# A layer norm, attention and int8 MLP block on one core: PV products of two key tiles at a time, two probability buffers, attended rows stored over the queries, and the output projection spread over the next batch's windows

## Chip, cores, metric

One NeuronCore of a Trainium2 chip runs one program. The metric is the device time of one execution in microseconds (us); three executions of the kernel before were timed, and one more was profiled. The engines are TensorE (PE in the rows; PEld is its weight loads), VectorE (DVE), ScalarE (ACT), GpSimd (POOL) and SyncE (SP), which issues the DMAs.

## What is computed

```python
x: (4, 512, 512) f32;  xn = layernorm(x)
# attention: 32 heads of 16, one key/value head shared by all
q = xn @ wq;  k = xn @ wk;  v = xn @ wv          # k, v: 16 wide
probs = softmax(causal(q @ k.T / 4))
s = (probs @ v) @ wo
# int8 MLP: columns of the input whose absolute maximum is over 3.0 stay out of the quantization;
# rows of the rest, and rows of W, are rounded to 127 steps of their own absmax
h = linear8bit(xn, W1, b1)                        # 512 -> 2048
g = silu(linear8bit(h, W2, b2))                   # 2048 -> 512
out = x + s * g
```

## The kernel before

All of it is one program with an instruction stream per engine, written out by hand; semaphores order them. An operand of a matmul that needs full precision is split into a high and a low half (fp32r), and a product is three matmuls: high by high, high by low, low by high. There are four stages.

1. Preparation (to about 92 us): layer norm, transposition of x, queries of all four batches into the tiles `big_h` and `big_l` (both halves, features by tokens, resident for the whole kernel), keys and values.
2. Attention (about 94 to 453 us), the stage of the change.
3. First MLP stage (L1046 on): W1 tiles are scaled, rounded and transposed; h = W1 by quantized x, in 16 feature tiles f of 4 chunks c of 512 tokens each. The quantized x overwrites `big_h` and `big_l`.
4. Second MLP stage and the output.

**Attention.** A unit u is one batch b and one strip f of 128 query features (8 heads of 16): U = 16 units, f = u mod 4. Time is counted in steps g (L747, L822, L961 loop over them on each engine), and CH = 24 steps make a window. Three things run staggered in it:
- Row maxima. `max_piece` (L878) computes the scores of unit u in 24 pieces, queries by keys, into three banks in turn; VectorE reduces each to its maxima (L838) and so frees the bank. After the 24th, `maxima` (L953) transposes the maxima into the miscellaneous bank MISCB (L957). ScalarE takes their high half (`mh`, L779), VectorE their low half (`ml`, L873), and SyncE puts both beneath the queries in `stack` (L660), so that the next score matmuls subtract the maxima.
- Scores and probabilities, one window later. `scores` (L901, L910) issues 22 matmuls per unit, keys by queries, 11 for each of two head parities p, with three banks; ScalarE takes the exponential into `probs` (L759), and GpSimd zeroes the masked corner after the last one of each key tile kt (L741). Key tile kt has 512 - 128 kt query columns.
- PV (L915, L922). Per parity and key tile, four matmuls with 32 weight columns each (values and ones) go side by side into the four column groups of the array and add into one bank, PVB, over the four key tiles. `PV_AT` says at which step of the unit each is issued. VectorE transposes the bank (L805, L811), takes reciprocals and transposes back (L819); GpSimd multiplies (L725). ScalarE and GpSimd store both halves of the attended rows (L767, L730) into `at_h`, `at_l`, which have five slots.

Since `probs` is one buffer, the exponentials of a parity wait for PV of the other parity before (L757).

**Output projection** (`project`, L938). For batch b, row tile j of 128 tokens is the sum over the four units k of the batch: three matmuls of 512 columns for each (j, k), a *projection step* below. Its bank is MISCB, the one that row maxima use; `misc_bank` (L927) has the first step of a row tile wait until the last user of the bank was taken: `maxima_low` (s_ml) after row maxima, `projected_evicted` (s_ob) after another row tile. `PROJECT_AT` (L556) lists the steps, counted from the batch's last unit; `PROJECT_LAST` that of the last batch, back to back after everything.

**The tail.** After the last piece (g = 384) tiles of the quantized x are loaded from DRAM (L680), transposed (L982) into the freed maxima banks, and their halves stored over the queries in `big_h`, `big_l` (L786, L852), every second step. EARLY = 15 of the 16 tiles are done so. The last one is done in the first MLP stage (`transpose_x` L1260, `high_x` L1117, `low_x` L1178) ahead of chunk 1 of f = 0.

In the first MLP stage the banks 4 to 7 serve all transposes in turn: `aux` (L1035) lists them, and the n-th waits until the one four before it was taken (`aux_bank`, L1252). In VectorE's order (L1213 on) come the low half of the first W1 tile, the scaling of the second, the scaling of W2's first 128 rows (`scale_w2`, L1186; a load of 1 MB), and then `low_x`. The code of the parts that the diff touches:

## Time and profile before

| | us |
|---|---|
| median of 3 executions | 870.93 (869.99 to 877.79) |
| profiled execution: time | 875.71 |
| profiled execution: span of its trace | 874.0 |
| TensorE busy (matmuls) | 799.8 (92%) |
| VectorE / ScalarE / GpSimd busy | 675.3 / 406.5 / 253.5 |
| mean granted TensorE clock | 0.966 of full speed |

Busy times are sums over the span; "idle before" in a row is the engine's idle time ahead of the instruction and what ended it. A matmul row's duration overlaps the next one's, so the cost of a matmul is read from its start to the next one's start. PEclk 1.00 is 2.4 GHz, 0.50 is 1.2 GHz.

### The profile page before, as it was taken

Reading aid. Unit: us, or ns where it says so; the run is one execution under the profiler, and the core shown is the slowest. Engines: PE = TensorE matmul, PEld = TensorE weight load, DVE = VectorE, ACT = ScalarE, POOL = GpSimd, SP = SyncE. Lnnn points to the kernel's source line nnn. Section 1 sums busy time; section 2 is a strip of 40 time slices with the busy share of each in tenths; the row PEclk is TensorE's granted clock in tenths of the full one; section 3 lists DMA queues with packets and bytes.
Section 4 is the critical chain, followed back from the end, with each engine's and each line's share of the span. In section 5 each row is a group of like instructions: output and inputs, shape, how many; then the busy total and the mean of one; then the engine's idle time right before and its main releaser. Section 6 shows DMA issues by size and latency. Waiting matters only on the chain. (4 is left out here: it accounts for less than half of the span.)

```text
span 874.0 us, 12108 instructions
## 1 busy us (share of the span) xinstructions
PE 799.8 (92%) x4253; PEld 579.6 (66%) x4253; DVE 675.3 (77%) x1116; ACT 406.5 (47%) x682; POOL 253.5 (29%) x331
## 2 busy tenths in 40 slices
PE   3899999999999999999889999999996999999983
PEld 2677655556655665566457878787875888887772
DVE  6898879897798789878535675765656998599967
ACT  2224056665666566666833455445444332143221
POOL 7101125454455445444441001010100000135306
PEclk9999679999999999999999999999997999999997
DMA  5721202322232222231534443412004234024852
GB/s 143 238 99 49 65 23 64 87 77 74 81 88 78 87 79 70 63 99 62 169 126 142 143 152 114 145 53 81 25 24 169 61 120 157 25 85 144 258 200 96
DMA packets 53884, 89.90 MB, mean 103 GB/s; under 512 B 10288, under 2 KB 18496, under 8 KB 52416
## 3 DMA queue, kind: packets, MB, share of 16 engines
q1 hardware_dynamic: 53824, 89.13, 32.6%
q8 instruction: 34, 0.56, 0.3%
q14 instruction: 26, 0.21, 0.1%
HBM read 47.69 MB, written 28.31 MB: 87 GB/s over the span
## 5 line engine op out<-in xcount | busy, mean ns | idle before, releaser
L838 DVE TENSOR_REDUCE rowmax<-ps 128x2 f32<-128x512 f32 (+3 forms) x384 | 215.5, 592 | 48.1 <-PE ps L897 46.4
L759 ACT ACTIVATE probs<-ps 128x512 f32<-128x512 f32 (+1 forms) x352 | 182.1, 559 | 115.2 <-PE ps L910 114.2
L897 PE MATMUL ps<-km,stack 128*128 128x256 f32 (+3 forms) x512 | 154.6, 357 | 2.4 <-PEq L171 1.9
L897 PEld LDWEIGHTS ps<-km,stack 128*128 128x128 f32 (+1 forms) x512 | 97.4, 200 | 71.0 <-DVE rowmax L838 44.4
L910 PE MATMUL ps<-stack,ks 128*128 128x512 f32 (+1 forms) x352 | 134.3, 389 | 9.6 <-DMA stack<-ml 9.6
L741 POOL TENSOR_SCALAR_AFFINE_SELECT probs<-probs 128x512 f32<-128x512 f32 x128 | 79.8, 635 | 115.5 <-ACT probs L759 115.5
L1631 PE MATMUL ps<-big_h 128*128 128x512 f32 x256 | 101.9, 398 | 9.1 <-DVE big_l L1556 9.1
L1303 PE MATMUL ps<-big_h,w1h 128*128 128x512 f32 x256 | 105.2, 411 | 1.4 <-DVE w1l L1174 1.4
L1305 PE MATMUL ps<-big_h,w1l 128*128 128x512 f32 x256 | 101.7, 397 | 0.0
L1304 PE MATMUL ps<-big_l,w1h 128*128 128x512 f32 x256 | 101.1, 395 | 0.0
L1633 PE MATMUL ps<-big_h,big_l 128*128 128x512 f32 x256 | 100.9, 394 | 0.0
L1632 PE MATMUL ps<-big_l,big_h 128*128 128x512 f32 x256 | 100.9, 394 | 0.0
L922 PE MATMUL ps<-probs,vones 128*32 128x512 f32 (+3 forms) x1024 | 95.5, 445 | 1.4 <-POOL probs L741 0.7
L910 PEld LDWEIGHTS ps<-stack,ks 128*128 128x128 f32 x352 | 66.9, 193 | 17.2 <-DMA stack<-ml 12.9
L1174 DVE TENSOR_TENSOR w1l<-ps,w1h 128x512 fp32r<-128x512 f32 x16 | 11.1, 692 | 71.2 <-ACT w1h L1114 71.2
L1631 PEld LDWEIGHTS ps<-big_h 128*128 128x128 f32 x256 | 48.8, 191 | 22.0 <-issue 11.9
L1491 ACT CAST big_h<-projected_rows 128x512 fp32r<-128x512 f32 x32 | 19.8, 618 | 88.1 <-DVE projected_rows L1529 65.2
L1305 PEld LDWEIGHTS ps<-big_h,w1l 128*128 128x128 f32 x256 | 48.4, 189 | 12.2
L1303 PEld LDWEIGHTS ps<-big_h,w1h 128*128 128x128 f32 x256 | 48.6, 190 | 11.7 <-DVE w1l L1174 1.6
L1633 PEld LDWEIGHTS ps<-big_h,big_l 128*128 128x128 f32 x256 | 48.8, 191 | 10.3
L1632 PEld LDWEIGHTS ps<-big_l,big_h 128*128 128x128 f32 x256 | 48.9, 191 | 10.0
L1304 PEld LDWEIGHTS ps<-big_l,w1h 128*128 128x128 f32 x256 | 48.6, 190 | 10.2
(193 smaller groups left out, 1286.1 us busy)
## 6 DMA issues: line engine op xcount, KB each, us to landing
stack<-big_h SPq DMA_DIRECT2D x128, 64.0 KB, 2.0
projected_rows<-w2t_scratch SPq DMA_DIRECT2D x32, 256.0 KB, 2.6
h_scratch<-hs SPq DMA_DIRECT2D x7, 1024.0 KB, 4.5
hload<-h_scratch SPq DMA_DIRECT2D x14, 512.0 KB, 5.0
xn_scratch<-xa SPq DMA_DIRECT2D x4, 1024.0 KB, 5.2
stack<-big_l SPq DMA_DIRECT2D x64, 64.0 KB, 2.0
xi<-xn_scratch SPq DMA_DIRECT2D x16, 256.0 KB, 2.7
xe_scratch<-xm SPq DMA_DIRECT2D x16, 256.0 KB, 2.3
```

The source lines that it names most:

```text
L741: nc.gpsimd.affine_select(out=d, in_=d, compare_op=ALU.is_ge, fill=0.0, base=0, pattern=[[0, NPAIR], [1, P]], channel_multiplier=-1).then_ ...
L759: nc.scalar.activation(probs[:, o:o + nh * w], ps[:, STB[n % NST], 0:nh * w], ACT.Exp).then_inc(s_exp, 1)
L838: nc.vector.tensor_reduce(dst, src, AX_X, ALU.max).then_inc(s_red, 1)
L897: last = nc.tensor.matmul(dst, stack[u % 3][rows, hp, P * qt:P * (qt + 1)], km[rows, u // KT, p0:p0 + npar, keys], start=True, stop=True)
L910: ins = nc.tensor.matmul(ps[:, STB[n % NST], 0:nh * w].rearrange("p (h q) -> p h q", h=nh), ks[:, u // KT, p, P * kt:P * (kt + 1)], stack[ ...
L922: ins = nc.tensor.matmul(ps[32 * j:32 * j + 32, PVB, P * kt:T], vones[:, u // KT, kt, :], probs[:, o:o + w], start=(kt == 0), stop=(kt == ...
L1303: nc.tensor.matmul(dst, w1h[f % 2][:, k, :], big_h[:, k, t], start=(k == 0), stop=False)
L1304: nc.tensor.matmul(dst, w1h[f % 2][:, k, :], big_l[:, k, t], start=False, stop=False)
L1305: last = nc.tensor.matmul(dst, w1l[f % 2][:, k, :], big_h[:, k, t], start=False, stop=(k == KT - 1))
L1631: nc.tensor.matmul(ps[:, i, :], hqh[m % RB][:, t], w2h[m % RB], start=(kk == 0), stop=False)
L1632: nc.tensor.matmul(ps[:, i, :], hqh[m % RB][:, t], w2l[m % RB], start=False, stop=False)
L1633: return nc.tensor.matmul(ps[:, i, :], hql[m % RB][:, t], w2h[m % RB], start=False, stop=(kk == FT - 1))
```

## The change

- PV takes two key tiles at a time: `GROUPS` = (0, 1), (2, 3). The eight issues of four matmuls per unit become four of eight, at steps 11, 16, 22, 27 of the unit where they were at 7, 11, 14, 16, 19, 21, 25, 27. The matmuls are the same.
- `probs` gets a second buffer, one for each parity; the exponentials wait for the PV of the same parity of the unit before.
- The attended rows are stored over the queries of their own unit in `big_h` and `big_l`; `at_h` and `at_l` go.
- The projection of batches 0 and 1 is spread over the four windows of the next batch, one row tile in each, at steps 3, 8, 13, 19 after T0. Batch 2 has its row tiles 0 and 1 in the last two windows with pieces, and its row tiles 2 and 3, every second step, in the tail.
- Because batch 3's attended rows stand where x tiles 12 to 15 would go, EARLY is 12: the tail does 12 tiles, and the first MLP stage four, two ahead of chunk 1 and two ahead of chunk 2. Their loads are issued two ahead of the weights' and two behind them.

The diff, cut to its core:

```diff
@@ tiles
-        probs = sa("probs", [P, NP_])
+        probs = [sa(f"probs{p}", [P, NP_]) for p in range(2)]
...
-        SLOTS = KT + 1
-        at_h = sa("at_h", [P, SLOTS, T], F32R)
-        at_l = sa("at_l", [P, SLOTS, T], F32R)
+        def attended(part, u):
+            b, f = divmod(u, KT)
+            return part[:, f, T * b:T * (b + 1)]
...
+        GROUPS = [(0, 1), (2, 3)]
+        NG = len(GROUPS)
@@ tables
-        PV_AT = {7: (0, 0), 11: (0, 1), 14: (0, 2), 16: (0, 3), 19: (1, 0), 21: (1, 1), 25: (1, 2), 27: (1, 3)}
+        PV_AT = {11: (0, 0), 16: (0, 1), 22: (1, 0), 27: (1, 1)}
...
-        T0 = CH + 11
-        PROJECT_AT = {t + T0: divmod(n, KT) for n, t in enumerate(
-            [-1, 1, 2, 3, 11, 12, 14, 15, 18, 20, 23, 24, 34, 35, 37, 39])}
+        T0 = 2 * CH + 2 - LAG
+        def spread_over(windows):
+            return {T0 + CH * w + at: (j, k) for j, (w, steps) in enumerate(windows) for k, at in enumerate(steps)}
+
+        EVENLY = (3, 8, 13, 19)
+        PROJECT_AT = spread_over([(j, EVENLY) for j in range(QT)])
+        PROJECT_NEXT_TO_LAST = spread_over([(0, EVENLY), (1, EVENLY), (2, (0, 2, 4, 6)), (2, (8, 10, 12, 14))])
...
-                table = PROJECT_AT if b + 1 < B else PROJECT_LAST
+                table = PROJECT_AT if b + 2 < B else PROJECT_NEXT_TO_LAST if b + 1 < B else PROJECT_LAST
...
-        EARLY = NT - 1
+        EARLY = NT - QT
@@ scalar, attention
-                        if 2 * u + p >= 1:
-                            act.wait_ge(s_pv, pv_count(u, p, kt) - 4)
+                        if u:
+                            act.wait_ge(s_pv, pv_count(u - 1, p, group_of(kt)))
...
-                        if u >= SLOTS:
-                            act.wait_ge(s_mf, misc_at[("o", (u - SLOTS) // KT, QT - 1)] + 1)
-                        nc.scalar.copy(at_h[:, u % SLOTS, :],
+                        nc.scalar.copy(attended(big_h, u),
@@ tensor, attention
-                def pv(u, p, kt):
-                    if kt == 0 and 2 * u + p:
+                def pv(u, p, group):
+                    if group == 0 and 2 * u + p:
                         pe.wait_ge(s_pvf, 2 * u + p)
-                    pe.wait_ge(s_msk, pv_count(u, p, kt))
-                    w = T - P * kt
-                    for j in range(NPAIR):
...
+                    for kt in GROUPS[group]:
+                        pe.wait_ge(s_msk, masked_count(u, p, kt))
+                        w = T - P * kt
+                        for j in range(NPAIR):
...
@@ first MLP stage
+        def late_x(f, c):
+            return range(EARLY + 2 * c - 2, EARLY + 2 * c) if f == 0 and c in (1, 2) else ()
...
-                if f == 0 and c == 1:
-                    aux += [("x", i) for i in range(EARLY, NT)]
+                aux += [("x", i) for i in late_x(f, c)]
...
-                for i in range(EARLY, NT):
-                    load_x(i)
+                load_x(EARLY)
+                load_x(EARLY + 1)
                 load_w1(1)
                 load_w1(2)
                 sp.dma_start(w2n[:, :], W2[0:P, :]).then_inc(s_w2n, 16)
+                for i in range(EARLY + 2, NT):
+                    load_x(i)
...
-                        if f == 0 and c == 1:
-                            for i in range(EARLY, NT):
-                                transpose_x(i)
+                        for i in late_x(f, c):
+                            transpose_x(i)
```

**Order of TensorE in a window of attention with projection.** Kernel before, from the first PV of the window (parity 1, key tile 0) on, two steps after the transposition of the row maxima; L897 is a piece, L910 a score matmul, L922 PV, L947 to L949 a projection step:

```order
L922 MATMUL ps<-probs,vones 32x512 [waits probs_masked,pv_bank_taken]
L922 MATMUL ps<-probs,vones 32x512 x3
L897 MATMUL ps<-km,stack 128x384 [waits max_reduced]
L910 MATMUL ps<-stack,ks 128x512 [waits exp_done]
L897 MATMUL ps<-km,stack 128x384 [waits max_reduced]
L910 MATMUL ps<-stack,ks 128x512 [waits exp_done]
L922 MATMUL ps<-probs,vones 32x384 [waits probs_masked]
L922 MATMUL ps<-probs,vones 32x384 x3
L897 MATMUL ps<-km,stack 128x256 [waits max_reduced,stack2_queries1]
L947 MATMUL ps<-woh,at_h 128x512 [waits attended_low,maxima_low]
L948 MATMUL ps<-wol,at_h 128x512
L949 MATMUL ps<-woh,at_l 128x512
```

The kernel after, same part of such a window, from the scores of the third step after that transposition on (L909 pieces, L922 scores, L935 PV, L960 to L962 projection):

```order
L922 MATMUL ps<-stack,ks 128x512 [waits exp_done]
L909 MATMUL ps<-km,stack 128x384 [waits max_reduced]
L922 MATMUL ps<-stack,ks 128x512 [waits exp_done]
L960 MATMUL ps<-woh,big_h 128x512 [waits attended_low,maxima_low]
L961 MATMUL ps<-wol,big_h 128x512
L962 MATMUL ps<-woh,big_l 128x512
L909 MATMUL ps<-km,stack 128x256 [waits max_reduced,stack0_queries1]
L935 MATMUL ps<-probs,vones 32x512 [waits probs_masked,pv_bank_taken]
L935 MATMUL ps<-probs,vones 32x512 x3
L935 MATMUL ps<-probs,vones 32x384 [waits probs_masked]
L935 MATMUL ps<-probs,vones 32x384 x3
L909 MATMUL ps<-km,stack 128x2x128 [waits max_reduced]
```

The first projection step of the row tile, which waits for the row maxima's low half, stood behind two PV issues and now stands ahead of the merged one.

**Order of TensorE at the last row maxima** (g = 385, the beginning of the tail). Before (L957 the maxima, L982 a tile of x):

```order
L957 MATMUL ps<-ident,rowmax 8x128 [waits projected_evicted,row_maxima_whole]
L957 MATMUL ps<-ident,rowmax 8x128 x3
L910 MATMUL ps<-stack,ks 128x384 [waits exp_done]
L982 MATMUL ps<-ident,tail_rows 128x128 [waits max_reduced,tail_rows_loaded0]
L982 MATMUL ps<-ident,tail_rows 128x128 x3
L910 MATMUL ps<-stack,ks 128x384 [waits exp_done]
L910 MATMUL ps<-stack,ks 128x512 [waits exp_done]
L922 MATMUL ps<-probs,vones 32x512 [waits probs_masked,pv_bank_taken]
L922 MATMUL ps<-probs,vones 32x512 x3
L982 MATMUL ps<-ident,tail_rows 128x128 [waits max_reduced,tail_rows_loaded1]
```

After (L970 the maxima, L995 a tile of x, L922 scores, L960 to L962 projection):

```order
L970 MATMUL ps<-ident,rowmax 8x128 [waits projected_evicted,row_maxima_whole]
L970 MATMUL ps<-ident,rowmax 8x128 x3
L922 MATMUL ps<-stack,ks 128x384 [waits exp_done]
L995 MATMUL ps<-ident,tail_rows 128x128 [waits max_reduced,tail_rows_loaded0]
L995 MATMUL ps<-ident,tail_rows 128x128 x3
L922 MATMUL ps<-stack,ks 128x384 [waits exp_done]
L960 MATMUL ps<-woh,big_h 128x512 [waits attended_low,maxima_low]
L961 MATMUL ps<-wol,big_h 128x512
L962 MATMUL ps<-woh,big_l 128x512
L922 MATMUL ps<-stack,ks 128x512 [waits exp_done]
L995 MATMUL ps<-ident,tail_rows 128x128 [waits max_reduced,tail_rows_loaded1]
L995 MATMUL ps<-ident,tail_rows 128x128 x3
```

A projection step that waits for the low half of those maxima has come between the second and the third score matmul.

**Order of TensorE in the first MLP stage, f = 0, up to chunk 2.** Before, from the last matmul of chunk 1 (L1303 to L1305 the products; L1272 transposes the second W1 tile):

```order
L1304 MATMUL ps<-big_l,w1h 128x512
L1305 MATMUL ps<-big_h,w1l 128x512
L1272 MATMUL ps<-ident,w1t_second 128x128 [waits w1_rounded]
L1272 MATMUL ps<-ident,w1t_second 128x128 x3
L1303 MATMUL ps<-big_h,w1h 128x512 [waits xe_low]
L1304 MATMUL ps<-big_l,w1h 128x512
L1305 MATMUL ps<-big_h,w1l 128x512
```

After (L1281 transposes tiles 14 and 15 of x, L1289 the second W1 tile, L1319 to L1321 the products):

```order
L1321 MATMUL ps<-big_h,w1l 128x512
L1281 MATMUL ps<-ident,projected_rows 128x128 [waits xe_loaded0]
L1281 MATMUL ps<-ident,projected_rows 128x128 x3
L1281 MATMUL ps<-ident,projected_rows 128x128 [waits xe_loaded1,w1_low]
L1281 MATMUL ps<-ident,projected_rows 128x128 x3
L1289 MATMUL ps<-ident,w1t_second 128x128 [waits w1_rounded,xe_low]
L1289 MATMUL ps<-ident,w1t_second 128x128 x3
L1319 MATMUL ps<-big_h,w1h 128x512 [waits xe_low]
L1320 MATMUL ps<-big_l,w1h 128x512
```

The transposition of the W1 tile now waits for `xe_low`, a low half of x. VectorE gives it; its order there before (L1188 to L1196 scale W2, L1181 is the low half of tile 15):

```order
L1188 TENSOR_REDUCE cst<-w2n 128x1 [waits w2_loaded]
L1191 TENSOR_SCALAR w_scale<-cst 128x1 [waits w2_scale_step]
L1194 RECIPROCAL cst<-w_scale 128x1 [waits w2_scale_step]
L1196 TENSOR_SCALAR w2n<-w2n,cst 128x2048 [waits w2_scale_step]
L1181 TENSOR_TENSOR big_l<-ps,big_h 128x4x128 [waits xe_high]
L1158 TENSOR_REDUCE cst<-w1n 128x1 [waits w1_loaded0]
```

and after (L1205 to L1213 scale W2, L1198 the low halves of tiles 12 to 15):

```order
L1205 TENSOR_REDUCE cst<-w2n 128x1 [waits w2_loaded]
L1208 TENSOR_SCALAR w_scale<-cst 128x1 [waits w2_scale_step]
L1211 RECIPROCAL cst<-w_scale 128x1 [waits w2_scale_step]
L1213 TENSOR_SCALAR w2n<-w2n,cst 128x2048 [waits w2_scale_step]
L1198 TENSOR_TENSOR big_l<-ps,big_h 128x4x128 [waits xe_high] x4
L1175 TENSOR_REDUCE cst<-w1n 128x1 [waits w1_loaded0]
```

Four low halves stand behind the scaling of W2, where there was one.

## Rows read from the trace of the kernel before

**Rows 1.** Windows of attention and its end; columns named in the first line
```profile
core 0: us, PE busy (x) PEld busy (x) DVE busy (x) ACT busy (x) POOL busy (x), PEclk, DMA share, GB/s
...
145.50:164.20 18.70, 17.57 (x123) 10.00 (x124) 17.22 (x36) 12.51 (x25) 10.13 (x14) 1.00 0.27 73
...
182.90:204.30 21.40, 20.36 (x137) 12.26 (x135) 17.35 (x36) 13.03 (x26) 10.13 (x14) 1.00 0.23 64
204.30:226.90 22.60, 22.60 (x147) 14.57 (x147) 17.51 (x35) 13.62 (x28) 9.91 (x13) 1.00 0.32 96
226.90:247.00 20.10, 19.95 (x136) 12.11 (x135) 17.46 (x36) 13.07 (x26) 9.41 (x13) 1.00 0.29 82
...
413.40:441.90 28.50, 24.22 (x187) 12.35 (x187) 16.09 (x29) 22.63 (x46) 12.34 (x17) 1.00 0.45 141
```

**Rows 2.** Groups of instructions: busy us, mean ns, idle before and its releaser
```profile
L838 DVE TENSOR_REDUCE rowmax<-ps 128x2 f32<-128x512 f32 (+3 forms) x384 | 215.5, 592 | 48.1 <-PE ps L897 46.4
L759 ACT ACTIVATE probs<-ps 128x512 f32<-128x512 f32 (+1 forms) x352 | 182.1, 559 | 115.2 <-PE ps L910 114.2
```

**Rows 3.** TensorE's timeline in a window with projection: start, duration, instruction
```profile
226.82 0.60 PE L957 MATMUL ps<-ident,rowmax 128*8 128x128 f32 x4
...
228.40 1.06 PE L922 MATMUL ps<-probs,vones 128*32 128x512 f32 x8
229.39 0.45 PE L897 MATMUL ps<-km,stack 96*128 96x384 f32 x1
...
230.09 0.39 PE L910 MATMUL ps<-stack,ks 128*128 128x512 f32 x1
230.41 0.85 PE L922 MATMUL ps<-probs,vones 128*32 128x384 f32 x8
231.19 0.50 PE L947 MATMUL ps<-woh,at_h 128*128 128x512 f32 x1
231.53 0.39 PE L948 MATMUL ps<-wol,at_h 128*128 128x512 f32 x1
231.76 0.39 PE L949 MATMUL ps<-woh,at_l 128*128 128x512 f32 x1
```

**Rows 4.** Timeline from row maxima to the next unit's first scores
```profile
182.86 0.60 PE L957 MATMUL ps<-ident,rowmax 128*8 128x128 f32 x4
...
185.47 0.66 DVE L873 TENSOR_TENSOR ml<-ps,mh 8x512 fp32r<-8x512 f32 x1
...
189.18 0.50 PE L910 MATMUL ps<-stack,ks 128*128 128x512 f32 x1 [0.98 <-DMA stack<-ml]
```

**Rows 5.** Timeline of the tail of attention
```profile
413.39 0.60 PE L957 MATMUL ps<-ident,rowmax 128*8 128x128 f32 x4
...
414.35 0.30 PEld L910 LDWEIGHTS ps<-stack,ks 128*128 128x128 f32 x2
...
416.90 0.67 DVE L873 TENSOR_TENSOR ml<-ps,mh 8x512 fp32r<-8x512 f32 x1
...
423.22 0.66 PE L982 MATMUL ps<-ident,tail_rows 128*128 128x128 f32 x4
...
423.63 0.59 PE L910 MATMUL ps<-stack,ks 128*128 128x384 f32 x2
```

**Rows 6.** Timeline of the first MLP stage, f = 0
```profile
464.55 2.29 DVE L1188 TENSOR_REDUCE cst<-w2n 128x1 f32<-128x2048 f32 x1 [4.08 <-DMA w2n<-in_L_ffn_W_dram]
...
468.46 0.68 DVE L1181 TENSOR_TENSOR big_l<-ps,big_h 128x512 fp32r<-128x512 f32 x1
...
469.20 0.50 PE L1303 MATMUL ps<-big_h,w1h 128*128 128x512 f32 x1
```

**Rows 7.** The stages' boundary and after it, by stretch (columns as in rows 1)
```profile
453.20:457.06 3.86, 0.63 (x4) 0.42 (x5) 0.69 (x1) 1.17 (x2) 1.80 (x1) 0.96 0.75 265
457.06:459.80 2.74, 2.74 (x7) 2.16 (x8) 1.09 (x4) 0.00 (x0) 0.00 (x0) 0.50 1.04 343
```

More of the change, by code:

```diff
@@ L611, in bank_of, with pv_count, masked_count, group_of @@
             return MAXB[use[2] - 1] if use[0] == "o" and use[1] == B - 1 and use[2] else MISCB
-        def pv_count(u, p, kt):
-            return 8 * u + 4 * p + kt + 1
+        def pv_count(u, p, group):
+            return NG * (2 * u + p) + group + 1
+        def masked_count(u, p, kt):
+            return QT * (2 * u + p) + kt + 1
+        def group_of(kt):
+            return next(n for n, kts in enumerate(GROUPS) if kt in kts)
         with nc.Block() as block:
@@ L729, in _ @@
                         pool.wait_ge(s_ah, u + 1)
-                        nc.gpsimd.tensor_tensor(at_l[:, u % SLOTS, :], tb[:, :, :].rearrange("p a b -> p (a b)"),
-                                                at_h[:, u % SLOTS, :].bitcast(F32), ALU.subtract).then_inc(s_al, 1)
+                        nc.gpsimd.tensor_tensor(attended(big_l, u), tb[:, :, :].rearrange("p a b -> p (a b)"),
+                                                attended(big_h, u).bitcast(F32), ALU.subtract).then_inc(s_al, 1)
                     u, s_ = scored(g)
@@ L737, in _ @@
                         w = T - P * kt
[L738 removed]
+                        d = probs[p][:, P_OFF[kt]:P_OFF[kt] + NPAIR * w].rearrange(
                             "p (h q) -> p h q", h=NPAIR)[:, :, 0:P]
@@ L801, in normalize @@
                     if part == 0:
-                        dve.wait_ge(s_pv, pv_count(u, 0, QT - 1))
+                        dve.wait_ge(s_pv, pv_count(u, 0, NG - 1))
                         if u:
@@ L807, in normalize @@
                     if part == 1:
-                        dve.wait_ge(s_pv, pv_count(u, 1, QT - 1))
+                        dve.wait_ge(s_pv, pv_count(u, 1, NG - 1))
                         if u:
@@ L945, in project @@
                     c = slice(P * j, P * (j + 1))
-                    slot = (KT * b + k) % SLOTS
-                    nc.tensor.matmul(dst, at_h[:, slot, c], woh[:, k, :], start=(k == 0), stop=False)
-                    nc.tensor.matmul(dst, at_h[:, slot, c], wol[:, k, :], start=False, stop=False)
-                    last = nc.tensor.matmul(dst, at_l[:, slot, c], woh[:, k, :], start=False, stop=(k == KT - 1))
+                    ah, al = attended(big_h, KT * b + k), attended(big_l, KT * b + k)
+                    nc.tensor.matmul(dst, ah[:, c], woh[:, k, :], start=(k == 0), stop=False)
+                    nc.tensor.matmul(dst, ah[:, c], wol[:, k, :], start=False, stop=False)
+                    last = nc.tensor.matmul(dst, al[:, c], woh[:, k, :], start=False, stop=(k == KT - 1))
                     if k == KT - 1:
@@ L968, in _ @@
                         scores(u, s_)
-                    for at, (p, kt) in PV_AT.items():
+                    for at, (p, group) in PV_AT.items():
                         if unit_at(g, at) >= 0:
-                            pv(unit_at(g, at), p, kt)
+                            pv(unit_at(g, at), p, group)
                     if projected(g)[0] >= 0:
@@ L1288, in _ @@
                     for c in range(NC):
-                        if f == 0 and c == 1:
-                            for i in range(EARLY, NT):
-                                transpose_x(i)
+                        for i in late_x(f, c):
+                            transpose_x(i)
                         if c == w2_chunk(f):
```

13 lines of the change are left out of this document (6 added, 7 removed).

## Prediction

> **What bounds the kernel now.** I read the slices by stretch first, then the waits, then single stretches of TensorE's timeline. In attention each unit (one batch, one strip of 128 query columns) takes one window of 24 steps, from one transposition of row maxima (L957) to the next; call its start M. The 15 windows from the first M, 107.6 us, to the last, 413.4 us, come in three kinds [rows 1]. Without output projection a window takes 18.7 us: VectorE is busy for 17.2 of it and TensorE 17.6. With four projection steps in it, it takes 21.4 or 20.1. With eight it takes 22.6 and TensorE is busy for all of it. So TensorE sets the windows full of projection, and VectorE's 24 score reductions, with the waits between the two engines, set the others. ScalarE waits 114.2 us in all, and for scores (L910), not for the attended product (L922) [rows 2]. So a second probability buffer by itself hides no wait; it only permits the later, merged product. In the two MLP stages TensorE is nearly always busy, and nothing touches them but their first microseconds.
>
> **Merging the PV products.** Eight short blocks of PV matmuls per window become four. A block of 512 columns takes 0.99 us from its start to the next matmul's (228.40 to 229.39), one of 384 takes 0.78 (230.41 to 231.19) [rows 3]. 128 columns are thus worth 0.21 us, and 0.14 us of each block is not columns. On entry the matmul before costs 0.32 us (230.09 to 230.41), where such a one costs 0.23 (231.53 to 231.76), so 0.09; on exit 0.34 (231.19 to 231.53), so 0.11. Entry and exit, 0.19 to 0.20, go with each block removed; of the 0.14 inside I let 0.08 go. That is 0.27 us for each of four blocks, 1.1 us per window, bounds 0.19 and 0.33. I see no reason for a loss inside the block: the same column groups go on with new weights. The Trainium skill, "TensorEngine Tiling (Array Packing)", Key Properties, says that changing the tiling mode, and not merely the tile, makes the array drain. By it all 0.33 would go, another 0.2 us per window; the rows give the entry and exit part, and the part between key tiles is in no row.
>
> **Windows without projection** (three of the kind today, four afterwards, since the one at 182.9 loses its projection). TensorE's need falls by 1.1 us, but the merged block (1.88 us, with the piece and scores of its step about 2.4 us) feeds VectorE nothing. VectorE has at most three banks outstanding, worth about 1.8 us of its reductions (592 ns each [rows 2]), so it starves some 0.5 to 1 us where before it starved in smaller pieces. Scores of the next unit also still wait for the row maxima's DMA: M to first score is 182.86 to 189.18, 6.3 us [rows 4]. I leave these windows at 18.7, bounds 18.2 and 19.3. The window at 182.9 goes from 21.4 to 18.7: 2.7 us gained.
>
> **Ten windows with projection** (204.3 to 413.4, today 209.1 us, 20.9 each [rows 1]). Today a batch's 16 steps fall into three windows as 4, 8, 4 and a fourth has none; afterwards every window has four. TensorE's own need is 22.6 minus 4 steps of 0.71 (three matmuls of 0.23 to 0.24; the one at 231.19 has the exit's 0.1 on top), minus 1.1 for the merging: 18.6 us. Yet a wait appears. The first projection step comes four steps after M and needs the shared bank, so it waits until the low half of the maxima is taken (L873): 185.47 + 0.66, that is 3.3 us after M [rows 4]. Today two PV blocks stand ahead of it, and it starts 4.4 us after M (226.82 to 231.19) without a wait [rows 3]. They now stand behind it. What TensorE has to do between M and that step is only 2.1 us (four transposes 0.35, and four steps of pieces and scores, 1.7 by their columns at 0.23 per 512). Behind the waiting step stand the next piece, the big block and the next unit's scores, so about 1.2 us is lost in each window. Then come the remaining 18.6 - 2.1 = 16.5 us, and some 0.5 us of waits for reductions before the second big block; today's window with four well placed steps has 0.4 (20.1 against 19.7) [rows 1]. Window: 3.3 + 16.5 + 0.5 = 20.3 us. Gain 209.1 - 203.0 = 6.1 us; bounds 19.8 and 20.8 per window, 11 and 1 us.
>
> **The end of attention** (413.4 to 441.9, 28.5 us). Eight projection steps of batch 2 move in, three tiles of x move out. The first of the eight waits for the same low half, which here is ready at 416.90 + 0.67, 4.2 us after 413.39; TensorE is there at about 414.6, after the second of the scores at 414.35 [rows 5]. So it stands still some 3 us with scores, tile 1 and PV behind it. SyncE's queue is held too (its load of tile 3 waits for tile 1), but it has ended before the scores need it. After the wait TensorE must do 8 x 0.71 of projection, 25 score matmuls (5.4 by their columns), 11 tiles of 0.41 (423.22 to 423.63, 4.5 [rows 5]) and three big and three small PV blocks (3 x 2.91): 24.3 us. With 4.2 in front that is 28.5. Waits I add as an estimate: 1 for the eviction between the two row tiles (two steps apart), 1 for tile loads in the last four tiles, which have no projection beside them, 0.3 at the last mask. 30.8 us: 2.3 lost, bounds 0 and 5. The last projection no longer waits for three tiles, 0.3 us gained.
>
> **The start of the first MLP stage.** It now transposes four tiles of x. Three more cost 3 x 0.41 [rows 5], and that is hidden by what follows. The larger price is a wait that the diff does not show. The transposed second weight tile takes the bank of tile 12, so it waits for that tile's low half, and in VectorE's order all low halves stand behind the scaling of W2, which starts at 464.55 when its 1 MB has landed. Today the one low half starts at 468.46, and only the fourth chunk (469.20) needs it. One more 256 KB load is ahead of W2, at the 343 GB/s of that stretch 0.8 us [rows 6, 7]. So the low half of tile 12 ends at 468.46 + 0.8 + 0.7 = 469.95, the weights are transposed by 470.35, and that chunk (12 matmuls, 2.8 us) and the transposes of W2 (0.45) give 473.6 for the fourth instead of 469.20: 4.4 us lost, bounds 3.5 and 5.5. Before it TensorE stands nearly still for over 4 us. After 3.9 us with 0.6 busy today it runs 2.74 us at clock 0.50, that is 1.2 GHz, and loses half of them [rows 7]: 1.3 us more, bounds 0 and 1.6. Afterwards TensorE is the bound, and nothing gives this back.
>
> **Sum.** -2.7 - 6.1 + 2.3 - 0.3 + 4.4 + 1.3 = -1.1 us. The profiled execution took 875.7 us (span 874.0), so 874.6. It is slower than the median of the runs shown, 870.9; the difference carried over gives 869.8.
>
> **Rivals.** *Faster.* If the low half of the maxima comes earlier (VectorE gets its pieces sooner once no PV block stands there) or the wait merely takes the place of today's wait for the maxima's DMA at the first score, as the 0.98 us there suggests [rows 4], the windows fall to need plus today's 0.4: 19.0. That is 10 x 1.9 + 2.7 = 21.7 gained and 7.7 lost, 856.9 us. Against it: the bound of the wait is a chain of three engines that the change does not shorten. Chance 0.25.
> *Slower.* The low half comes later than 3.3 us after M. Each 0.1 us costs ten windows 1 us. In the tail it already takes 4.2. ScalarE's copy of the high half stands behind exponentials, and VectorE's behind reductions, and both will now be fed in bursts. From 4.3 us on the kernel is slower by over 1%; at 4.5 it takes 869.8 + 12 = 882. For it: 4.2 exists. Against it: in the windows shown it is 3.3. Chance 0.12.
> *The merging doesn't do what it says.* If the array empties between two key tiles as between two blocks, 0.27 becomes 0.05 and a projection window 21.2: 0.22 x 4 x 10, 9 us more, 878.6. Nothing in the trace shows two key tiles in a row. Chance 0.08.
> *The clock.* The wait of 3 us in the tail could also end in 1.2 GHz, as the idle 3.9 us do today; again 1.3 us, 871.1. Chance 0.10. The Trainium skill, "TensorE: Matmul & The Clock Gate", section on HAM oscillation, says that waits between bursts of matmuls send the engine back to half rate, so that each restart is paid for. By it both waits would count.
>
> **How the numbers follow.** My forecast has 0.45. About 1%, 8.7 us, is what a measurement of this kernel can tell from no change. Faster by more: 0.25 (the first rival). Slower by more: 0.12 (the second). Within: 0.45 + 0.08 + 0.10 = 0.63. Range: ends of the windows (5 us either way), of the tail (2 to 3), of the MLP's start (2 down, 1 up), not all at once, 860 to 880.
>
> **What would show it.** Right: windows without projection at 18.7 and all ten others between 19.8 and 20.8; the first projection matmul of a row tile 3.3 us after M with a wait for the low half named ahead of it or before its weights; a PV block of 512 and 384 columns about 1.7 us long; 30 to 31 us from the last M to the last PV; TensorE idle ahead of the second weight transposition of the MLP, some 3 us, and clock 0.50 behind it. Wrong: windows at 19 or at 21.5, a low half before 2.5 us or after 4; no wait ahead of the weight transposition.

## The result, and the profile after

| | median of 20 runs, us | lowest to highest |
|---|---|---|
| before | 871.88 | 869.76 to 877.79 |
| after | 876.60 | 871.11 to 881.05 |

The ratio is 1.0048, 95% interval 1.0034 to 1.0063. The kernel became slower by half a per cent (the medians differ by 4.7 us), where a gain of 1.1 us was forecast. The profiled execution of the kernel after took 878.58 us, with a span of 876.9 (874.0 before). In the kernel after, the row maxima are transposed on L970, the scores are L922, the pieces L909, PV L935, the first projection matmul L960, the low half of the maxima L885, a tile of x in the tail L995.

The stretches of the kernel after that answer to [rows 1], with its columns: one window without projection, one with, all ten with projection together, and the end of attention.

```profile
145.31:164.20 18.89, 17.33 (x125) 10.28 (x124) 17.13 (x36) 12.21 (x25) 10.31 (x14) 1.00 0.27 72
222.29:242.69 20.40, 19.61 (x137) 12.44 (x134) 17.38 (x36) 13.00 (x27) 9.89 (x13) 1.00 0.28 81
201.89:406.11 204.22, 196.16 (x1340) 123.81 (x1337) 174.09 (x350) 129.55 (x260) 99.11 (x131) 1.00 0.27 77
406.11:440.57 34.46, 28.51 (x200) 17.54 (x200) 15.48 (x27) 22.38 (x46) 12.83 (x17) 0.95 0.40 117
```

The ten projection windows take 204.2 us (209.1 before), and the window that lost its projection takes 18.8 like its neighbours. From the first row maxima to the last it is 298.5 us where it was 305.85: 7.3 gained. Then the end of attention takes 34.5 where it took 28.5: 5.95 lost. The MLP's first product stands at 455.69 and the first of the fourth chunk at 471.28, 15.6 us, where it was 12.1 (457.06 to 469.20 [rows 6, 7]): 3.45 lost. These three make +2.1 us. The remaining 0.8 of the 2.9 us in span lies in the rest of the MLP stages, from the fourth chunk to the end: 404.8 us before, 405.6 after. No edit of this document touches them, and yet they took between 400.8 and 405.6 us in the eleven profiled executions. So a difference of 2.9 us between two spans is no larger than this spread; the ratios of the medians and the single stretches are what to go by.

Two groups of the page after, against [rows 2]:

```profile
L850 DVE TENSOR_REDUCE rowmax<-ps 128x2 f32<-128x512 f32 (+3 forms) x384 | 211.6, 590 | 42.5 <-PE ps L909 41.1
L774 ACT ACTIVATE probs<-ps 128x512 f32<-128x512 f32 (+1 forms) x352 | 179.3, 558 | 113.7 <-PE ps L922 112.5
```

Durations are the same, and ScalarE still waits for scores and not for PV. What stalls TensorE is seen in the timeline of a projection window, against [rows 3]:

```profile
222.29 0.60 PE L970 MATMUL ps<-ident,rowmax 128*8 128x128 f32 x4
...
225.61 0.50 PE L960 MATMUL ps<-woh,big_h 128*128 128x512 f32 x1 [0.51 <-DVE ml L885]
...
226.42 0.28 PE L909 MATMUL ps<-km,stack 128*128 128x256 f32 x1
226.63 1.71 PE L935 MATMUL ps<-probs,vones 128*32 128x512 f32 x16
228.27 0.74 PE L909 MATMUL ps<-km,stack 96*128 96x256 f32 x3
```

The first projection step stands 3.3 us after the maxima (222.29 to 225.61) and waits for their low half; the merged PV block comes behind it and takes 1.64 us to the next matmul. At the last maxima the same wait is longer, and a drop of the clock follows:

```profile
406.11 0.60 PE L970 MATMUL ps<-ident,rowmax 128*8 128x128 f32 x4
...
408.99 0.69 DVE L864 TENSOR_TENSOR big_l<-ps,big_h 128x512 fp32r<-128x512 f32 x1 [2.20 <-ACT big_h L798]
409.60 0.67 DVE L885 TENSOR_TENSOR ml<-ps,mh 8x512 fp32r<-8x512 f32 x1
...
410.32 0.50 PE L960 MATMUL ps<-woh,big_h 128*128 128x512 f32 x1 [2.82 <-DVE ml L885]
...
420.45 0.51 PE L960 MATMUL ps<-woh,big_h 128*128 128x512 f32 x1 [0.55 <-ACT projected_rows L638]
...
426.26 0.66 PE L995 MATMUL ps<-ident,tail_rows 128*128 128x128 f32 x4 [0.68 <-DMA tail_rows<-xe_scratch]
...
434.54 0.66 PE L995 MATMUL ps<-ident,tail_rows 128*128 128x128 f32 x4 [1.45 <-DMA tail_rows<-xe_scratch]
```

These rows also show why the low half comes later here than in a window: in VectorE's order the low half of the tail's first x tile (L864) stands ahead of it, and VectorE stood idle for 2.20 us until ScalarE had given that tile's high half. ScalarE had given the high half of the maxima, which L885 needs, at about 408.5, so up to 1.1 us of the wait may come from this order. No run here moved it.

The same stretch by windows; the last number but two is the granted clock (0.50 is 1.2 GHz, 1.00 is 2.4 GHz):

```profile
405.82:410.30 4.48, 1.58 (x18) 1.06 (x10) 2.26 (x5) 2.67 (x6) 0.84 (x2) 1.00 0.36 117
410.30:412.00 1.70, 1.68 (x9) 1.45 (x10) 0.72 (x2) 0.44 (x1) 0.00 (x0) 0.92 0.00 0
412.00:415.00 3.00, 3.00 (x14) 2.08 (x13) 1.34 (x3) 1.83 (x4) 0.74 (x2) 0.50 0.38 97
```

In the first MLP stage, against [rows 6]: the transposition of the second W1 tile (L1289) waits for the first of four low halves (L1198), which stand behind the scaling of W2 (L1205 to L1213).

```profile
455.69 0.50 PE L1319 MATMUL ps<-big_h,w1h 128*128 128x512 f32 x1 [1.40 <-DVE w1l L1191]
...
462.99 2.29 DVE L1205 TENSOR_REDUCE cst<-w2n 128x1 f32<-128x2048 f32 x1 [1.93 <-DMA w2n<-in_L_ffn_W_dram]
...
466.90 2.48 DVE L1198 TENSOR_TENSOR big_l<-ps,big_h 128x512 fp32r<-128x512 f32 x4
467.64 0.66 PE L1289 MATMUL ps<-ident,w1t_second 128*128 128x128 f32 x4 [1.97 <-DVE big_l L1198]
...
471.28 0.48 PE L1319 MATMUL ps<-big_h,w1h 128*128 128x512 f32 x1
```

Behind that wait the clock stays at 1.00:

```profile
467.64:471.28 3.64, 3.64 (x20) 3.05 (x21) 3.40 (x7) 0.15 (x1) 0.06 (x1) 1.00 0.02 5
```

### The profile page after: what moved, and what is told of

It reads as the page before. It is cut to its first block and busy times, and to the rows that moved or that the text cites. A ratio compares the mean times of both kernels' runs of the same rounds, so it can differ in the third digit from the quotient of the medians.

```text
span 876.9 us, 12083 instructions
## 1 busy us (share of the span) xinstructions
PE 795.4 (91%) x4253; PEld 585.4 (67%) x4253; DVE 674.2 (77%) x1116; ACT 404.9 (46%) x682; POOL 253.3 (29%) x331
## 3 DMA queue, kind: packets, MB, share of 16 engines
q1 hardware_dynamic: 53824, 89.13, 32.8%
## 5 line engine op out<-in xcount | busy, mean ns | idle before, releaser
L850 DVE TENSOR_REDUCE rowmax<-ps 128x2 f32<-128x512 f32 (+3 forms) x384 | 211.6, 590 | 42.5 <-PE ps L909 41.1
L774 ACT ACTIVATE probs<-ps 128x512 f32<-128x512 f32 (+1 forms) x352 | 179.3, 558 | 113.7 <-PE ps L922 112.5
L909 PE MATMUL ps<-km,stack 128*128 128x256 f32 (+3 forms) x512 | 156.5, 359 | 8.1 <-DVE rowmax L850 4.7
L909 PEld LDWEIGHTS ps<-km,stack 128*128 128x128 f32 (+1 forms) x512 | 95.9, 200 | 69.5 <-DVE rowmax L850 34.5
L922 PE MATMUL ps<-stack,ks 128*128 128x512 f32 (+1 forms) x352 | 135.2, 388 | 4.7 <-DMA stack<-ml 4.5
L1319 PE MATMUL ps<-big_h,w1h 128*128 128x512 f32 x256 | 105.0, 410 | 1.4 <-DVE w1l L1191 1.4
L1321 PE MATMUL ps<-big_h,w1l 128*128 128x512 f32 x256 | 101.8, 398 | 0.0
L935 PE MATMUL ps<-probs,vones 128*32 128x512 f32 (+3 forms) x1024 | 82.3, 439 | 0.1
L922 PEld LDWEIGHTS ps<-stack,ks 128*128 128x128 f32 x352 | 67.4, 192 | 10.7 <-DMA stack<-ml 6.3
L1507 ACT CAST big_h<-projected_rows 128x512 fp32r<-128x512 f32 x32 | 19.8, 618 | 88.4 <-DVE projected_rows L1545 65.6
L1321 PEld LDWEIGHTS ps<-big_h,w1l 128*128 128x128 f32 x256 | 48.4, 189 | 12.2
L1319 PEld LDWEIGHTS ps<-big_h,w1h 128*128 128x128 f32 x256 | 48.6, 190 | 11.6 <-DVE w1l L1191 1.6
L1320 PEld LDWEIGHTS ps<-big_l,w1h 128*128 128x128 f32 x256 | 48.6, 190 | 10.3
```

What stands on the lines that cost most here:

```text
L774: nc.scalar.activation(probs[p][:, o:o + nh * w], ps[:, STB[n % NST], 0:nh * w], ACT.Exp).then_inc(s_exp, 1)
L850: nc.vector.tensor_reduce(dst, src, AX_X, ALU.max).then_inc(s_red, 1)
L909: last = nc.tensor.matmul(dst, stack[u % 3][rows, hp, P * qt:P * (qt + 1)], km[rows, u // KT, p0:p0 + npar, keys], start=True, stop=True)
L922: ins = nc.tensor.matmul(ps[:, STB[n % NST], 0:nh * w].rearrange("p (h q) -> p h q", h=nh), ks[:, u // KT, p, P * kt:P * (kt + 1)], stack[ ...
L935: ins = nc.tensor.matmul(ps[32 * j:32 * j + 32, PVB, P * kt:T], vones[:, u // KT, kt, :], probs[p][:, o:o + w], start=(kt == 0), stop=(kt ...
L1319: nc.tensor.matmul(dst, w1h[f % 2][:, k, :], big_h[:, k, t], start=(k == 0), stop=False)
```

## Experiments

All on the kernel after, unless said; each ratio is to the kernel before on the same chip. "The ten windows" are those with projection.

**The tail: is it the first projection step that costs?**

```diff
-  PROJECT_NEXT_TO_LAST = spread_over([..., (2, (0, 2, 4, 6)), (2, (8, 10, 12, 14))])
+  PROJECT_NEXT_TO_LAST = spread_over([..., (2, (4, 5, 6, 7)), (2, (10, 11, 12, 14))])
```

> Edit: in the tail the four steps of row tile 2 of batch 2 stand at 4, 5, 6, 7 instead of 0, 2, 4, 6, those of row tile 3 at 10, 11, 12, 14 instead of 8, 10, 12, 14; all else is the kernel after the change. Theory A (the wait for the low half of the last maxima, 3 us, and the half clock it brings, about 1.5 us, are what lengthens the tail): the tail, from the last row maxima to the first step of the last projection, falls from 34.5 us to 30 to 31.5, no wait of over 1 us for the low half, PEclk 1.00 all through, whole kernel 3 to 4.5 us faster than after the change. Rival B (it is the 5.7 us of work of eight more steps, wherever they stand): the tail stays above 33.5 us.

Measured 870.67 us, ratio 0.9983 (0.9967 to 0.9999). The end of attention by windows, and its timeline:

```profile
405.94:435.82 29.88, 26.40 (x200) 16.50 (x200) 15.19 (x27) 21.98 (x46) 12.76 (x17) 1.00 0.43 134
```

```profile
409.87 0.66 PE L995 MATMUL ps<-ident,tail_rows 128*128 128x128 f32 x4 [1.39 <-DMA tail_rows<-xe_scratch]
410.45 1.71 PE L935 MATMUL ps<-probs,vones 128*32 128x512 f32 x16
412.09 0.50 PE L960 MATMUL ps<-woh,big_h 128*128 128x512 f32 x1
```

29.9 us where it was 34.5, with the clock at 1.00 and no wait for the low half: with scores, tiles and PV ahead of it, the step finds it ready. A wait for a tile's load (L995) takes 1.4 back. The edit moves all eight steps, not only the first, so the wait for the eviction between the two row tiles goes with it; its 0.55 us are not separated from the rest. The tail is 4.6 us shorter than after the change and 2.7 shorter than in the next experiment, which has the same wait at full clock. The ratios differ by 5.7 us, more than theory A's 3 to 4.5. (The two profiled spans differ by 10.3 us, but 4.9 of that lies in the later stages that no edit touches.) This edit alone turns the slowdown into a time just below that of before.

**The MLP's start: low halves of two tiles ahead of the scaling of W2.**

```diff
   scale_w1(1)
+  for i in late_x(0, 1):
+      low_x(i)
   scale_w2(0)
...
-  for i in range(EARLY, NT):
+  for i in late_x(0, 2):
```

> Edit: in the first MLP stage VectorE takes the low halves of x tiles 12 and 13 ahead of the scaling of W2, those of 14 and 15 behind it as before; all else is the kernel after the change. Theory A (the second W1 tile's transposition waits for a bank that tile 12 holds until W2 is scaled): the wait of 2 us ahead of that transposition goes, the fourth chunk starts 12.5 to 13.5 us after the first instead of 15.6, the kernel is 2 to 3 us faster than after the change. Rival B (it is the loads of tiles 14 and 15, or the W2 load, that set it): the fourth chunk still starts over 15 us after the first, since W2 scaled is needed by it anyway (there 12.1 us in the kernel before).

Measured 873.40 us, ratio 1.0014 (1.0000 to 1.0028). Timeline of VectorE and TensorE there:

```profile
459.88 1.29 DVE L1198 TENSOR_TENSOR big_l<-ps,big_h 128x512 fp32r<-128x512 f32 x2 [0.73 <-ACT big_h L1138]
...
461.08 2.28 DVE L1205 TENSOR_REDUCE cst<-w2n 128x1 f32<-128x2048 f32 x1
...
462.99 0.60 PE L1291 MATMUL ps<-ident,w1t_second 128*128 128x128 f32 x4
```

The transposition has no wait ahead of it, W2's scaling is not delayed, and the fourth chunk starts after 12.5 us where it was 15.6. By the ratios the kernel is 3.0 us faster than after the change, as theory A had it. In this execution the tail took 32.5 us with the same wait of 2.8 but at full clock:

```profile
406.43:438.96 32.53, 26.96 (x199) 16.51 (x199) 15.56 (x27) 22.19 (x46) 12.74 (x17) 1.00 0.42 123
```

**The same from the other side: twelve early tiles on the kernel before.** Its last four tiles are loaded, cast and transposed in the MLP stage as in the kernel after, and nothing else is changed.

```diff
-  EARLY = NT - 1
+  EARLY = NT - QT
```

(and the loops over `range(EARLY, NT)` split over chunks 1 and 2 as in the change)

> Edit: on the kernel before, only EARLY = 12 and the tiles of x two and two in the first MLP stage; attention, its projection and buffers as before. Theory A (the bank wait comes from this part of the change alone): the fourth chunk starts 15 to 17.5 us after the first instead of 12.1, the tail loses 0.5 to 2 us of its 28.5, in all 1.5 to 4 us slower than before. Rival B (the wait needs the late loads that the rest of the change brings): fourth chunk within 13 us.

Measured 875.49 us, ratio 1.0045 (1.0029 to 1.0060). The end of attention is only 1.5 us shorter (27.0), and the fourth chunk starts after 16.7 us instead of 12.1:

```profile
463.78 1.29 DVE L1200 TENSOR_SCALAR w2n<-w2n,cst 128x2048 f32<-128x2048 f32 x1
464.98 2.48 DVE L1185 TENSOR_TENSOR big_l<-ps,big_h 128x512 fp32r<-128x512 f32 x4
465.72 0.76 PE L1276 MATMUL ps<-ident,w1t_second 128*128 128x128 f32 x4 [2.58 <-DVE big_l L1185]
```

```profile
463.00:466.00 3.00, 0.42 (x5) 0.28 (x4) 2.90 (x6) 0.64 (x2) 0.00 (x0) 1.00 0.00 0
466.00:469.00 3.00, 3.00 (x11) 2.44 (x10) 2.90 (x7) 0.00 (x0) 0.00 (x0) 0.52 0.02 5
```

Here the wait is followed by a clock of 0.52, as my forecast had it. Theory A held. This part alone makes the kernel as much slower as the whole change does.

**The first projection step of a window two steps later**, behind the merged block.

```diff
-  EVENLY = (3, 8, 13, 19)
+  EVENLY = (5, 9, 14, 19)
```

> Edit: the four projection steps of a window stand at 5, 9, 14, 19 instead of 3, 8, 13, 19, so the first follows the merged PV block instead of standing ahead of it; all else is the kernel after the change. Theory A (the wait for the low half mostly takes the place of the wait for the maxima's DMA, which sets the next unit's first score at 6.3 us after the maxima): the wait for the low half goes, a wait of 0.5 to 1 us for the DMA comes back, windows go from 20.4 to 20.0 to 20.3 us only, kernel 1 to 4 us faster. Rival B (the wait for the low half is lost whole): windows fall by its 0.8 to 1.2 us to 19.2 to 19.6, kernel 8 to 12 us faster.

Measured 870.85 us, ratio 0.9968 (0.9946 to 0.9990). The ten windows:

```profile
201.31:401.17 199.86, 194.43 (x1340) 125.40 (x1337) 172.59 (x350) 127.76 (x260) 99.13 (x131) 1.00 0.28 79
```

The waits in that stretch of the kernel after, then of this one (engine, line waited for, total us, times, longest):

```profile
PEld ps L960 <- DVE ml L885: 8.8, 10, 0.9
PE ps L960 <- DVE ml L885: 5.1, 10, 0.5
```

```profile
PEld ps L922 <- DMA stack<-ml: 5.6, 10, 0.6
```

The wait for the low half is gone from all ten windows, and another has come at the first score of the next unit, for the maxima's DMA. Of the 1.2 us that I had put down as lost at the first wait (3.3 less 2.1 of work), the window gives back 0.4 (204.2 to 199.9 for ten); 0.6 is now the wait for the DMA, and 0.2 are not located. So the windows went as theory A had it, but by the ratios the kernel is 7 us faster than after the change, where theory A had 1 to 4. In the profiled execution 4.4 of it stands in the windows and 1.7 in the tail, which was at full clock again (32.8); the MLP's start had a low one behind its wait and took 17.1, 1.5 more. What makes up the rest is not shown.

**The old projection table** (4, 8, 4 and none), batch 2's included, with all else as after.

```diff
-  PROJECT_AT = spread_over([(j, EVENLY) for j in range(QT)])
+  PROJECT_AT = {t + T1: divmod(n, KT) for n, t in enumerate(
+      [-1, 1, 2, 3, 11, 12, 14, 15, 18, 20, 23, 24, 34, 35, 37, 39])}
...
-  table = PROJECT_AT if b + 2 < B else PROJECT_NEXT_TO_LAST if b + 1 < B else PROJECT_LAST
+  table = PROJECT_AT if b + 1 < B else PROJECT_LAST
```

> Edit: the projection's table of the kernel before (4, 8, 4 and no steps in the four windows, nothing of batch 2 in the tail) in the kernel after the change; merged PV, two buffers, rows over the queries and twelve tiles stay. Theory A (spreading gains in the windows and loses in the tail): windows of a batch about 18.8, 21.0, 21.5 to 22, 19.6 (sum 81 to 82.5 against 81.6 evenly spread), tail 26.5 to 28 us instead of 34.5; in all 5 to 7 us faster than after the change, so 1 to 3 us faster than before it. Rival B (spreading is what gains in the windows): windows sum to 83 or more per batch and eat half of what the tail gives back.

Measured 878.99 us, ratio 1.0068 (1.0047 to 1.0089), the slowest of all. The ten windows:

```profile
203.85:413.89 210.04, 199.44 (x1352) 127.63 (x1349) 170.52 (x350) 129.78 (x262) 99.09 (x130) 1.00 0.27 79
```

The same ten windows of the kernel before:

```profile
204.24:413.39 209.15, 203.30 (x1349) 124.09 (x1349) 175.25 (x350) 130.97 (x262) 98.41 (x130) 1.00 0.28 79
```

210.0 us against 209.1 before and 204.2 after: the spread table brings the whole gain of the windows, and with the old table merging and the second buffer bring none. (The spread table alone, on the kernel before, was not run.) Theory A, 5 to 7 us faster than after the change, was wrong. The tail gives back 7.4 us (27.1 instead of 34.5), but from the first row maxima to the last it is 307.0 us instead of 298.5, 8.5 more: 5.8 in the ten windows, most of the rest (2.5) in the window that has its projection steps again. TensorE is busy for 3.9 us less than before (199.4 against 203.3), and waits for more than that.

**PV one key tile at a time**, in the eight places of before.

```diff
-  GROUPS = [(0, 1), (2, 3)]
+  GROUPS = [(0,), (1,), (2,), (3,)]
...
-  PV_AT = {11: (0, 0), 16: (0, 1), 22: (1, 0), 27: (1, 1)}
+  PV_AT = {7: (0, 0), 11: (0, 1), 14: (0, 2), 16: (0, 3), 19: (1, 0), 21: (1, 1), 25: (1, 2), 27: (1, 3)}
```

> Edit: PV in eight issues per unit at the steps of the kernel before; two buffers, spreading, rows over the queries and twelve tiles stay as after the change. Theory A (two PV blocks ahead of the first projection step hide the wait for the low half, and VectorE starves less): a window with projection needs 19.7 us of TensorE and takes 19.9 to 20.2, so less than the 20.4 with merging, and one without takes 18.7. The merging, which takes 0.55 us of TensorE's time off a window, then gains nothing. Rival B (the merging gains what it takes off TensorE): windows with projection 20.8 to 21.0, without 18.9 or more.

Measured 872.67 us, ratio 1.0019 (1.0002 to 1.0035). The ten windows, and TensorE at the start of one:

```profile
201.31:403.74 202.43, 198.28 (x1340) 122.26 (x1338) 173.22 (x351) 130.89 (x260) 99.12 (x131) 1.00 0.27 78
```

```profile
221.57 0.60 PE L970 MATMUL ps<-ident,rowmax 128*8 128x128 f32 x4
...
223.15 1.06 PE L935 MATMUL ps<-probs,vones 128*32 128x512 f32 x8
...
225.17 0.85 PE L935 MATMUL ps<-probs,vones 128*32 128x384 f32 x8
225.95 0.50 PE L960 MATMUL ps<-woh,big_h 128*128 128x512 f32 x1
```

Ten windows take 1.8 us less than with merged PV (20.2 each, the end of theory A's range), and those without projection 18.7 instead of 18.9. Two PV blocks fill the time until the low half is there, and the projection step starts 4.4 us after the maxima without a wait. Merging took this filling away and put it behind the wait.

**One probability buffer instead of two**, the exponentials waiting for the PV group just before.

```diff
-  probs = [sa(f"probs{p}", [P, NP_]) for p in range(2)]
+  probs = [sa("probs", [P, NP_])] * 2
...
-  if u:
-      act.wait_ge(s_pv, pv_count(u - 1, p, group_of(kt)))
+  if 2 * u + p >= 1:
+      act.wait_ge(s_pv, pv_count(u, p, group_of(kt)) - NG)
```

> Edit: one probability buffer for both parities, the exponentials wait for the PV group of the parity before; all else as after the change. Theory A (the second buffer is needed for merged PV at step 11, since the exponentials of steps 11 to 14 and of the next unit's first steps would wait for it): windows 0.3 to 1 us longer, 5 to 12 us in all. Rival B (ScalarE runs far enough behind TensorE that it costs nothing): windows as after, 18.8 and 20.4.

Measured 874.32 us, ratio 1.0036 (1.0022 to 1.0050), not slower than the kernel after. The ten windows take 204.0, so theory A (0.3 to 1 us more in each) was wrong. ScalarE does wait for PV now, and it costs nothing:

```profile
ACT probs L774 <- PE ps L922: 61.6, 60, 3.4
...
ACT probs L774 <- PE ps L935: 7.9, 10, 0.8
```

Its waits for scores shrink by about as much (70.8 in the ten windows of the kernel after).

**The three moves together** (first, second and fourth experiment).

> Edit: the three moves together (tail steps later, low halves of tiles 12 and 13 first, first step of a window later), on the kernel after the change. Theory A (the three losses are separate): windows 20.0, tail 30, fourth chunk 12.5 us after the first; against the kernel after that is 4 + 4.6 + 3.1, some 11 to 12 us faster, 864 to 866 us, 6 to 8 faster than before. Rival B (they share a cause, the tail or the MLP's start gets back what the windows gain, as in the run with the first step later, whose fourth chunk came 17.1 us after the first): under 8 us faster than after.

Measured 863.99 us, ratio 0.9921 (0.9907 to 0.9936), while the kernel before took 871.36 on that chip. It has the lowest ratio of all and beats both kernels. By the ratios it is 11 us faster than the kernel after, as theory A had it: the three losses are separate. The ten windows and the tail:

```profile
200.87:400.66 199.79, 194.44 (x1340) 125.47 (x1337) 173.00 (x350) 127.81 (x260) 99.31 (x131) 1.00 0.28 79
400.66:430.44 29.78, 26.41 (x199) 16.53 (x200) 15.19 (x27) 21.96 (x46) 12.75 (x17) 1.00 0.47 135
```

The fourth chunk starts 13.6 us after the first product, where 12.5 was expected. No wait stands ahead of the weight transposition; but the clock is at 0.50 for the first 5.6 us of the stage, where in the kernel with that move alone it was for 3.0; half of the 2.6 between them is 1.3 us.

**The three moves with PV one key tile at a time.** The edits are those of the kernel just above and of "PV one key tile at a time".

> The kernel with the three moves (the table of the last batch, the low halves ahead of the W2 scaling, the first projection step later), but with PV of one key tile at a time in eight blocks instead of four. Theory A (scores wait on exponentials, TensorE has slack in a window even with the projection late enough): merging is worth nothing here either; the ten projection windows take 19.8 to 20.1 us against 20.0, the windows without projection 18.6 to 18.8, and the time is within 1.5 us of the same kernel with merged PV (864.0 us, ratio 0.992), so 862.5 to 865.5. Rival B (once the wait at the first projection step is gone, TensorE bounds the window, and the four blocks saved at 0.19 to 0.33 us each count in full): projection windows of 20.8 to 21.3 us, 8 to 13 us more in all, about 872 to 877.

Measured 865.45 us, ratio 0.9927 (0.9904 to 0.9950).

```profile
201.95:403.98 202.03, 198.07 (x1339) 121.29 (x1336) 171.62 (x351) 130.69 (x260) 98.87 (x131) 1.00 0.28 78
```

The total is within the 1.5 us that theory A allowed, and the ratios of the two can't be told apart. In the windows neither theory holds: they take 20.2, above A's 19.8 to 20.1 and far below B's 20.8. With the projection behind the PV block, merging gains 2.2 us in ten windows (202.0 to 199.8); with the projection ahead of it, it lost 1.8. Where the rest of its saving goes can be seen in TensorE's timeline, in the kernel with the three moves and merged PV:

```profile
222.54 0.39 PE L922 MATMUL ps<-stack,ks 128*128 128x512 f32 x1
223.02 0.44 PE L909 MATMUL ps<-km,stack 96*128 96x384 f32 x1
223.30 0.40 PE L922 MATMUL ps<-stack,ks 128*128 128x512 f32 x1
```

From the first of these to the next matmul it is 0.48 us, where one of 512 columns takes 0.23 when nothing holds up its successor (as in [rows 3]). I read the 0.25 us between them as a wait too short to be named in the row and partly counted as busy. With single blocks a score matmul at this place is followed after 0.24 us, or after 0.32 where a PV block comes next.

## Why the prediction was wrong

The direction was wrong, by terms that were mis-sized in a balance of nearly equal gains and losses. Forecast -1.1, measured in the profiled spans +2.9: the end of attention is off by +3.65, the windows by +1.5, the last projection by +0.3, the MLP's start by -2.25, and 0.8 lies in stages that the change does not touch.

- **The end of attention, +2.3 forecast, +5.95 measured. This step failed.** The first part of it held: the low half comes 4.2 us after the maxima, and TensorE stands still 2.8. Of the 3.65 that were missing, 1.6 to 1.9 is the clock (34.5 against 32.8 and 32.5 in two executions with the same wait at full clock). I had "again 1.3 us" as a rival with a chance of 0.10. It fell in the profiled execution after (0.50 from 412 to 415, the row above), and in those with PV one key tile at a time (34.7) and with one buffer (35.5), and not in two others with the same wait (32.5 and 32.8). Where the first step was moved behind other work, the tail took 29.8 to 29.9 and the clock stayed at 1.00, in all three executions. The other 1.7 is TensorE's work and waits beside the clock: without the drop, TensorE is busy for 26.96 us and idle for 5.6. I had 24.3 behind the front part, where some 25.4 is right if 1.5 of the busy time lies in front; how much of that 1.1 is work and how much waits too short to be named is not shown. The waits behind it are 2.8 instead of 2.3, most of them for tile loads.
- **The projection windows, 20.3 forecast, 20.4 measured.** The bound "3.3 us after M" was right to 0.1 us, and so was its cause, two PV blocks that no longer stand ahead. The bounds 19.8 and 20.8 held for every window (20.1 to 20.6). But the price of the wait was not right. I had it at 1.2 us a window; moved away, it gives back 0.4, since the window takes 20.0 then and not the 19.1 that need and waits gave. The number is right in part by luck.
- **Windows without projection: 18.7 forecast, 18.8 to 18.9 measured**, the lost 0.1 to 0.2 appearing only with merged PV (18.7 with single blocks). I had the gain of 1.1 us at the merged block given back whole, to VectorE's starvation. That it is given back was right, and slightly too little; that it is VectorE that takes it is not shown by itself.
- **Merging, 0.27 us a block.** The size was right or a little low: in the kernel before two blocks that took 0.99 and 0.78 take 1.64 together in the kernel after, two that took 0.57 and 0.35 (to 245.34 and to 246.54) take 0.79 (241.56 to 242.35), so 0.13 inside each, besides the entry and exit of 0.19. That is 0.32 a block, the upper bound. The rule of the Trainium skill, "TensorEngine Tiling (Array Packing)", Key Properties, that only a change of the mode drains the array, fits this better than my 0.27; the rival that merging does nothing for a block is refuted. But the 1.3 us of TensorE's time are not 1.3 us of a window. The window gives nearly all of them back as waits: with merging it is 0.2 us shorter or 0.2 longer, depending on where the projection stands. I had subtracted 1.1 us for it in full from "TensorE's own need" (18.6), which is why that need stands so far below the 20.0 that a window takes without the wait.
- **The last projection: 0.3 gained forecast, nothing measured** (15.16 before, 15.13 after).
- **The MLP's start, +5.7 forecast, +3.45 measured.** The mechanism held: the shared bank makes the weight transposition wait for VectorE's order. W2 did not come 0.8 us later: its reduction starts 7.3 us after the first product, 7.5 before; and half clock behind the wait, 1.3 us of my 5.7, did not happen in this execution (1.00 from 467.64 on). In the one with twelve tiles on the kernel before it did, and there the term is 4.6 us.
- **The second buffer** was costed at nothing, and is worth nothing.
- **The rivals.** The faster one (windows of 19.0) fell: with the wait for the low half moved away, windows still take 20.0, and a wait of 0.6 us for the maxima's DMA stands there instead. The slower one (low half at over 4.3 us) fell too, in the windows it stays at 3.3. What turned the forecast gain into a loss was the clock rival and the work and waits of the tail. The Trainium skill, "TensorE: Matmul & The Clock Gate", in its section on HAM oscillation, warned of a restart paid at half rate after waits between bursts, for waits that are longer than those here; the traces agree for a part of the executions only. Of the five that have the wait in the tail three show clock 0.50 behind it and two 1.00, and of the seven that have it ahead of the weight transposition four and three.

The choice that decided was to charge the clock in full at the wait in the MLP and to leave it as a rival of 0.10 at the wait in the tail. Charged at both, with the 1.6 to 1.9 us that it measured in the tail, the forecast would have been +0.5 to +0.8; with the work and waits of the tail that were read too lightly, about +2.5. Even that would have leaned on the 1.3 us in the MLP, which the profiled execution did not show.

## What to carry to other kernels

Before a step that waits for a value is moved forward, look for what stands ahead of it today and fills that time: here two PV blocks filled a wait of about 1.2 us, and merged behind it they cost ten windows 1.8 us more than single ones ahead of it. Work that shares a rotating buffer with other work inherits the order of the engine that releases it; moving three tiles cost 3.5 us through a bank that the diff doesn't mention. Where a change spreads load evenly over windows, take its ends from their own timeline: the tail alone cost 6.0 us of the 7.3 that the windows gained.

## What the runs showed of the hardware that was not expected

A wait of 2.8 us in the tail, with 1.4 to 1.6 us of matmuls in the 4.3 before its end, was followed by a granted clock of 0.50 in three executions and of 1.00 in two, of kernels with the same order of work in that stretch. With the low clock the tail took 34.5 to 35.5 us, without it 32.5 to 32.8, so it is worth 1.7 to 3 us. It begins at different moments, too. In the kernel after it begins at about 411.7, 1.4 us behind the wait's end (worked out from the 0.92 of the row from 410.30 to 412.00). In the one with one buffer the first projection matmul, at 410.35, already finds it:

```profile
410.40:412.00 1.60, 1.60 (x4) 1.31 (x5) 0.64 (x2) 0.00 (x0) 0.00 (x0) 0.50 0.00 0
```

What decides it is open; no run here varied it by itself.

PV blocks that follow each other with new weights in the same column groups cost no more than their columns: 0.21 us for 128 columns in merged blocks (1.64 less 0.79 for 512) as in single ones (0.99 less 0.57 for 256).
